# Scan convolutions on GpSimd and paired sampling weights in a four-stage vision kernel

## The chip, the cores and the metric

The kernel runs on one core of a Trainium2 chip. A core has TensorE (PE in the profile; PEld is its weight load), VectorE (DVE), ScalarE (ACT), GpSimd (POOL) and SyncE (SP), each with a queue of its own that it works through in order. They meet at semaphores only. Matrix products go to PSUM, eight banks of 512 float32 columns on 128 partitions; everything else lies in SBUF. GpSimd cannot read PSUM. The metric is device time in microseconds.

## The reference

Sixteen images of 64 channels and 16x16 pixels pass four layers, one after the other:

- L0: attention over channels. With q, k, v as 1x1 convolutions, `attn = softmax(scale * q @ k.T)` is 64x64 per image.
- L1: a modulated deformable 3x3 convolution. A 3x3 convolution gives two offsets and a mask for each of nine taps and each pixel; the image is sampled bilinearly at the shifted places, weighted with the mask and the convolution's weights, then batch norm and ReLU.
- L2: attention over the 256 pixels with a residual: `softmax(q.T @ k / 8)`, 256x256 per image.
- L3: a norm over the image, a 3x3 depthwise convolution giving `y`, then four scans added up, each `conv5(y) * sigmoid(g @ y)`: a depthwise convolution of five taps along rows (left to right, right to left) or along columns (both ways); a 1x1 convolution `fuse` with a residual; a second norm and a gated feed-forward layer with a residual.

## The kernel before

Images are worked in eight pairs n = 1 to 8, image 0 of a pair on partitions 0 to 63 and image 1 on 64 to 127, 256 pixels along the columns. All five engines' orders are written out by hand in `PLAN` (L53): a list of tokens `step.pair` for each of TensorE, ScalarE, VectorE and GpSimd, which `walk` (L147) plays in that order. Steps of up to four or five pairs are interleaved: while pair 4 is sampled, pair 1 is in its scans. A step waits for semaphores and issues its instructions. `turn` (L152) makes the users of a shared PSUM bank wait for the one before in the order of TensorE's list; bank `pair` (two banks) is used by wx, logit, gate, scan and ff, bank `mb` by the other small products.

The steps that the text names, by line:

- Front: qk, attn, at, mix and x1 are layer 0; x1 ends on VectorE in `x1_pad` (L863) and GpSimd copies it (L1033). off and off_t give the offsets, dist (L872), abs, hat (L877) and hat_y (L885) make triangular weights from them on VectorE and ScalarE; `high` (ScalarE) and `low` (GpSimd, L1039, five instructions) split them into two float16 parts, which tr0 to tr2 turn over on TensorE. wx0 to wx2 multiply the image with the convolution's weights.
- Sampling, nine taps per pair, 72 in all. `sp{k}` (L494, L489) spreads the row weights of a tap to PSUM bank yb0 (upper half of the image) and, for the tap before it, to yb1 (lower half), and the column weights to xb. ScalarE copies xb to SBUF (`xe`, L740). VectorE multiplies: `w{k}a` and `w{k}b` (L901), one instruction of 512 columns for each half of each tap, into a ring of six tiles. `s{k}a`, `s{k}b` (L534) multiply that with w_x into bank cv. After the last tap ScalarE's relu (L747) gives x2.
- Layer 2: qk2 (L547), v2, logit, max (L907), exp, nrm (L920), et, av, x3.
- Layer 3: st1 on VectorE and ln1 on GpSimd (five instructions on one column each, L1046 to L1055) make the norm, ScalarE writes `z_pad` (L785) and the first two depthwise taps, VectorE the other seven (dw2 to dw8, L942), and y (L951) adds the two sums into `y_pad`. gate (L602) and scan (L615) are TensorE's: the scan multiplies shifted views of `y_pad` with diagonal matrices, 2 axes x 5 taps x 2 images = 20 products, each two records in the trace. ScalarE adds the bias to `conv` (L808), prod (L957) multiplies with the gates, fuse, x4, st2, ln2, ff, u (L976), ff2 and out end the pair.
- `warm` and `hot` (L374, L380) are products of zeros, two per count, that keep TensorE at work at the start and after the last sampling.

Of the kernel before, what the change touches and what calls it, by code (L numbers as in the profile page):

```python
# [44 lines left out]
for _name, _n in PARTS:  # L45
# [29 lines left out]
        scan.5 sp3.8 tr2.8 s1a.8 qk2.7 s1b.8 sp4.8 s2a.8 fuse.5 sp5.8 logit.7 s2b.8 sp6.8 s3a.8 s3b.8 s4a.8 v2.7 s4b.8
        s5a.8 s5b.8 s6a.8 sp7.8 ff.5 et1.7 sp8.8 s6b.8 gate.6 et0.7 sp_last.8 s7a.8 av.7 s7b.8 s8a.8 s8b.8 ff2.5 scan.6
        qk2.8 hot.1 logit.8 fuse.6 hot.2 hot.3 v2.8 hot.4 et0.8 gate.7 et1.8 av.8 scan.7 hot.5 ff.6 fuse.7 gate.8 hot.6
        scan.8 ff2.6 hot.7 fuse.8 ff.7 hot.8 ff.8 ff2.7 hot.9 ff2.8
    """,
    "act": """  # L80
        attn.1 at.1 mix.1 off.1 prep.1 tanh.1 abs.1 attn.2 wx0.1 high.1 wx2.1 at.2 wx1.1 mix.2 tr0.1 xe0.1 tr1.1 xe1.1
        tr2.1 wx2.2 xe2.1 attn.3 halve.1 off.2 at.3 xe3.1 xe4.1 abs.2 mix.3 tanh.2 wx0.2 xe5.1 high.2 xe6.1 xe7.1 xe8.1
        tr0.2 attn.4 tr1.2 xe0.2 tr2.2 at.4 wx1.2 xe1.2 off.3 mix.4 relu.1 wx2.3 abs.3 wx0.3 tanh.3 xe2.2 xe3.2 high.3
        wx1.3 xe4.2 q2.1 k2.1 xe5.2 tr0.3 xe6.2 tr1.3 xe7.2 attn.5 xe8.2 tr2.3 xe0.3 v2.1 exp0.1 off.4 at.5 exp1.1 abs.4
        tanh.4 xe1.3 mix.5 xe2.3 et0.1 relu.2 wx0.4 et1.1 xe3.3 xe4.3 high.4 wx1.4 q2.2 k2.2 wx2.4 ln1.1 xe5.3 xe6.3
        dw.1 tr0.4 exp0.2 exp1.2 xe7.3 et0.2 xe8.3 v2.2 et1.2 tr1.4 xe0.4 xe1.4 tr2.4 gate.1 xe2.4 ln1.2 off.5 dw.2
        xe3.4 relu.3 scan.1 xe4.4 q2.3 k2.3 tanh.5 wx1.5 wx2.5 abs.5 wx0.5 xe5.4 ln2.1 high.5 v2.3 xe6.4 exp0.3 exp1.3
        xe7.4 tr0.5 ff.1 xe8.4 et1.3 gate.2 xe0.5 et0.3 xe1.5 tr1.5 ln1.3 relu.4 dw.3 attn.6 scan.2 q2.4 k2.4 xe2.5
        xe3.5 at.6 mix.6 tr2.5 exp0.4 exp1.4 xe4.5 wx2.6 off.6 xe5.5 ln2.2 wx1.6 v2.4 xe6.5 ff.2 abs.6 xe7.5 et0.4
        tanh.6 wx0.6 high.6 et1.4 xe8.5 tr0.6 gate.3 ln1.4 xe0.6 dw.4 scan.3 attn.7 tr1.6 xe1.6 relu.5 at.7 xe2.6 gate.4  # L90
        ln2.3 q2.5 k2.5 xe3.6 xe4.6 mix.7 scan.4 tr2.6 ff.3 xe5.6 off.7 abs.7 v2.5 xe6.6 tanh.7 wx0.7 high.7 xe7.6 wx1.7
        attn.8 wx2.7 xe8.6 tr0.7 at.8 mix.8 tr1.7 exp0.5 tr2.7 exp1.5 xe0.7 off.8 et0.5 xe1.7 relu.6 et1.5 xe2.7 wx0.8
        xe3.7 tanh.8 abs.8 wx2.8 ln1.5 q2.6 k2.6 xe4.7 wx1.8 dw.5 xe5.7 high.8 xe6.7 exp0.6 exp1.6 tr0.8 xe7.7 v2.6
        ln2.4 xe8.7 et1.6 xe0.8 et0.6 ff.4 xe1.8 relu.7 xe2.8 gate.5 ln1.6 dw.6 xe3.8 tr1.8 scan.5 xe4.8 q2.7 k2.7 tr2.8
        xe5.8 xe6.8 xe7.8 exp0.7 exp1.7 ln2.5 v2.7 ff.5 et1.7 xe8.8 et0.7 gate.6 ln1.7 relu.8 dw.7 scan.6 q2.8 k2.8
        exp0.8 v2.8 exp1.8 et0.8 et1.8 gate.7 ln2.6 ln1.8 dw.8 scan.7 ff.6 gate.8 ln2.7 scan.8 ff.7 ln2.8 ff.8
    """,
    "dve": """
        qk.1 a_max.1 a_norm.1 x1.1 dist.1 qk.2 a_max.2 hat.1 hat_y.1 a_norm.2 qk.3 low.1 x1.2 w0a.1 w0b.1 a_max.3 w1a.1
        a_norm.3 w1b.1 w2a.1 dist.2 w2b.1 w3a.1 hat.2 w3b.1 w4a.1 hat_y.2 x1.3 w4b.1 w5a.1 qk.4 w5b.1 w6a.1 w6b.1 w7a.1  # L100
        a_max.4 w7b.1 a_norm.4 w8a.1 w8b.1 w0a.2 dist.3 x1.4 w0b.2 w1a.2 hat.3 qk.5 hat_y.3 w1b.2 w2a.2 w2b.2 w3a.2
        w3b.2 w4a.2 w4b.2 w5a.2 a_max.5 w5b.2 w6a.2 w6b.2 w7a.2 max.1 a_norm.5 w7b.2 w8a.2 nrm0.1 dist.4 w8b.2 w0a.3
        nrm1.1 hat.4 w0b.3 w1a.3 hat_y.4 w1b.3 w2a.3 w2b.3 x3.1 st1.1 w3a.3 w3b.3 w4a.3 x1.5 w4b.3 w5a.3 max.2 dw3.1
        dw5.1 w5b.3 nrm0.2 w6a.3 nrm1.2 w6b.3 dw7.1 w7a.3 dw2.1 dw4.1 dw6.1 w7b.3 w8a.3 dw8.1 y.1 w8b.3 w0a.4 x3.2 st1.2
        w0b.4 w1a.4 w1b.4 w2a.4 dw2.2 dw4.2 dw6.2 dw8.2 dw3.2 dw5.2 dw7.2 dist.5 prod.1 w2b.4 y.2 x4.1 st2.1 w3a.4 hat.5
        hat_y.5 w3b.4 w4a.4 max.3 w4b.4 w5a.4 w5b.4 w6a.4 nrm1.3 nrm0.3 w6b.4 u.1 w7a.4 out.1 w7b.4 w8a.4 w8b.4 w0a.5
        x3.3 st1.3 qk.6 dw3.3 dw2.3 a_max.6 dw5.3 dw4.3 dw6.3 a_norm.6 dw7.3 w0b.5 w1a.5 prod.2 w1b.5 w2a.5 max.4 x1.6
        dw8.3 x4.2 st2.2 w2b.5 w3a.5 y.3 nrm0.4 w3b.5 w4a.5 dist.6 w4b.5 w5a.5 nrm1.4 u.2 w5b.5 hat.6 hat_y.6 out.2
        w6a.5 w6b.5 x3.4 st1.4 w7a.5 w7b.5 w8a.5 dw2.4 dw3.4 dw5.4 dw4.4 dw7.4 dw6.4 qk.7 dw8.4 y.4 a_max.7 prod.3 w8b.5
        w0a.6 a_norm.7 x4.3 st2.3 w0b.6 w1a.6 w1b.6 w2a.6 w2b.6 x1.7 w3a.6 w3b.6 u.3 w4a.6 out.3 dist.7 w4b.6 w5a.6  # L110
        hat.7 hat_y.7 qk.8 w5b.6 w6a.6 a_max.8 a_norm.8 max.5 w6b.6 w7a.6 w7b.6 x1.8 w8a.6 nrm0.5 prod.4 nrm1.5 w8b.6
        w0a.7 w0b.7 w1a.7 x3.5 dist.8 st1.5 x4.4 w1b.7 w2a.7 hat.8 w2b.7 w3a.7 hat_y.8 st2.4 w3b.7 w4a.7 max.6 w4b.7
# [1046 lines left out]
```

## Time and profile before

| | us |
|---|---|
| median of 3 runs (303.65, 303.65, 304.49) | 303.65 |
| span of the profiled execution, first to last instruction (the profile has no other time of it) | 301.8 |
| TensorE busy | 287.8 (95%) |
| VectorE busy | 213.0 (71%) |
| ScalarE busy | 190.4 (63%) |
| GpSimd busy | 53.0 (18%) |

Busy time is the union of an engine's instructions; TensorE's matmuls overlap and their ends are modelled, so the mean duration of one times the count is more than the busy time. An arrow in brackets behind an instruction names what ended the idle time before it. The share of the whole span hides that the first 28 and the last 46 us differ from the middle.

### The profile page before, as it was taken

What the parts mean: (1) busy time and instruction counts of PE and PEld (TensorE: products, weight loads), DVE (VectorE), ACT (ScalarE), POOL (GpSimd) and SP (SyncE); (2) the same over time, 40 slices, a digit from 0 to 9 for tenths busy, and PEclk for the clock granted to TensorE, in tenths of its full rate; (3) what the DMA queues carried; (4) which work ended last, traced back from release to release, by engine and by line L of the source; (5) the groups of instructions that cost most, each with busy time, mean ns of one, the idle gap of its engine ahead of it and who ended that gap; (6) DMA issues with size and microseconds to landing.
All of it is one profiled execution on the core that took longest, in us unless ns stands there. A gap on an engine that the chain in (4) does not pass through costs nothing.

```text
span 301.8 us, 7399 instructions
## 1 busy us (share of the span) xinstructions
PE 287.8 (95%) x2870; PEld 183.7 (61%) x2870; DVE 213.0 (71%) x424; ACT 190.4 (63%) x399; POOL 53.0 (18%) x139
## 2 busy tenths in 40 slices
...
DMA packets 3057, 4.98 MB, mean 16 GB/s; under 512 B 336, under 2 KB 2768, under 8 KB 2896
## 3 DMA queue, kind: packets, MB, share of 16 engines
...
HBM read 3.47 MB, written 1.05 MB: 15 GB/s over the span
## 4 chain that ended last, share of the span: by engine, by line
PE 85%; DVE 5%; ACT 5%; issue 3%; POOL 1%; ACTq 0%; POOLq 0%; DVEq 0%
PE ps_cv L534 22%; PE ps_pair L615 11%; PE ps_yb L494 8%; PE ps_pair L480 7%; PE ps_ma L437 6%; PE ps_ma L464 4%; PE ps_mb L580 3%; PE ps_pair L602 3%; PE ps_pair L570 3%; PE ps_mb L591 3%; PE ps_mb L547 3%; PE ps_mb L388 2%; PE ps_pair L635 2%; PE ps_mb L624 2%; PE ps_yb L374 1%
## 5 line engine op out<-in xcount | busy, mean ns | idle before, releaser
L901 DVE TENSOR_TENSOR sb_wt<-ps_yb,sb_xe 128x512 f32<-128x512 f32 x144 | 94.0, 684 | 26.4 <-PE ps_xb L489 24.9
L534 PE MATMUL ps_cv<-sb_wt,sb_w_x 128*64 128x256 f32 x576 | 77.3, 385 | 0.0
L740 ACT ACTIVATE sb_xe<-ps_xb 128x512 f32<-128x512 f32 x72 | 43.0, 597 | 19.3 <-PE ps_xb L489 19.2
L534 PEld LDWEIGHTS ps_cv<-sb_wt,sb_w_x 128*64 128x64 f32 x576 | 38.2, 136 | 20.2 <-issue 7.5
L615 PE MATMUL ps_pair<-sb_y_pad,sb_par 64*128 64x256 f32 x320 | 37.4, 383 | 0.3 <-ACT sb_gates L799 0.3
L615 PEld LDWEIGHTS ps_pair<-sb_y_pad,sb_par 64*128 64x128 f32 x320 | 30.9, 184 | 5.8 <-issue 2.5
L942 DVE SCALAR_TENSOR_TENSOR sb_dw_acc<-sb_z_pad,sb_par,sb_dw_acc 128x256 f32<-128x256 f32 x56 | 25.2, 480 | 9.4 <-ACT sb_dw_acc L792 5.3
L494 PE MATMUL ps_yb<-sb_hats,sb_sel 32*128 32x512 f16 x144 | 29.8, 383 | 0.7
L1039 POOL TENSOR_TENSOR sb_parts<-sb_hat,sb_parts 128x256 f16<-128x256 f32 (+2 forms) x40 | 23.3, 615 | 38.7 <-ACT sb_parts L710 38.6
L1046 POOL TENSOR_SCALAR sb_sc<-sb_mv 128x1 f32<-128x1 f32 x16 | 3.0, 190 | 142.1 <-DVE sb_mv L936 74.7
L489 PE MATMUL ps_xb<-sb_hats,sb_sel 32*128 32x512 f16 x72 | 27.7, 385 | 0.2 <-ACT sb_hats L719 0.2
L730 ACT ACTIVATE sb_w_x<-ps_pair 128x1024 f32<-128x1024 f32 (+1 forms) x24 | 19.4, 810 | 7.7 <-PE ps_pair L480 7.5
L480 PE MATMUL ps_pair<-sb_par,sb_x 64*128 64x256 f32 (+1 forms) x192 | 23.4, 361 | 0.6 <-ACT sb_w_x L730 0.3
L719 ACT ACTIVATE sb_hats<-ps_ma 128x1024 f16<-128x1024 f16 (+1 forms) x24 | 21.1, 880 | 1.7 <-PE ps_ma L464 1.5
L494 PEld LDWEIGHTS ps_yb<-sb_hats,sb_sel 32*128 32x128 f16 x144 | 7.3, 91 | 21.2 <-issue 17.0
L480 PEld LDWEIGHTS ps_pair<-sb_par,sb_x 64*128 64x128 f32 x192 | 15.5, 185 | 7.3 <-issue 6.7
L808 ACT ACTIVATE sb_conv<-ps_pair,sb_par 128x512 f32<-128x512 f32 x16 | 10.1, 683 | 13.1 <-PE ps_pair L615 13.0
L437 PE MATMUL ps_ma<-sb_x_pad,sb_par 128*64 128x128 f32 x288 | 17.4, 274 | 0.3 <-ACT sb_hats L719 0.3
L437 PEld LDWEIGHTS ps_ma<-sb_x_pad,sb_par 128*64 128x64 f32 x288 | 15.8, 136 | 2.3 <-issue 1.6
L769 ACT ACTIVATE sb_b_exp<-ps_pair,sb_b_neg 128x256 f32<-128x256 f32 x32 | 14.8, 473 | 3.0 <-DVE sb_b_neg L910 2.7
L872 DVE TENSOR_TENSOR sb_dist<-ps_ma,sb_grid 128x1152 f32<-128x1152 f32 x8 | 10.8, 1354 | 6.2 <-PE ps_ma L446 6.2
L464 PE MATMUL ps_ma<-sb_sel,sb_parts 128*64 128x128 f16 x320 | 13.8, 222 | 0.0
...
## 6 DMA issues: line engine op xcount, KB each, us to landing
...
sb_x_in<-in_x SPq DMA_DIRECT2D x8, 128.0 KB, 2.1
out_y<-sb_y_out SPq DMA_DIRECT2D x8, 128.0 KB, 1.7
...
sb_par<-in_par SPq DMA_DIRECT2D x1, 128.0 KB, 2.2
sb_sel<-in_sel SPq DMA_DIRECT2D x1, 128.0 KB, 3.9
```

The costliest lines, as they stand in the source:

```text
L437: mm = nc.tensor.matmul(ma[C * h:C * (h + 1), 0:P], par_sb[:, a + 2 * OM * t:a + 2 * OM * (t + 1)], x1_pad[:, r:r + HALF_ROWS, t % 3:t % 3 ...
L464: mm = nc.tensor.transpose(bk[columns_of(t), at:at + P], parts[:, 2 * h + b, 4 * g + 2 * t:4 * g + 2 * (t + 1), :, :], ident16)
L480: mm = nc.tensor.matmul(pair[:, 512 * b + PIX * h:512 * b + PIX * h + k], x1[r, P * h:P * (h + 1)], par_sb[r, a:a + k], start=True, stop=True)
L489: return nc.tensor.matmul(xb[:, :], sel_sb[rows, P:2 * P], hats[n % 2][rows, g, :], start=True, stop=True)
L494: return nc.tensor.matmul(yb[h][:, :], sel_sb[rows, P * (2 + h):P * (3 + h)], hats[n % 2][rows, g, :], start=True, stop=True)
L534: mm = nc.tensor.matmul(cv[C * b:C * (b + 1), 0:PIX], w_x[n % 2][:, b, h, k, :], wt_of(n, k, h)[:, PIX * b:PIX * (b + 1)], start=(k == 0 a ...
L615: mm = nc.tensor.matmul(pair[:, 512 * b + PIX * d:512 * b + PIX * (d + 1)], par_sb[r, a:a + P], rows, start=(j == 0), stop=(j == KS - 1))
L719: nc.scalar.activation(hats[n % 2][:, g0:g1, :].rearrange("p g q -> p (g q)"), ma[:, :].bitcast(F16)[:, 0:k], ACT.Copy).then_inc(ev(f"hats ...
L740: nc.scalar.activation(xe[t % XE][:, :], xb[:, :], ACT.Copy).then_inc(ev("xe_ok"), 1)
L901: nc.vector.tensor_tensor(wt_of(n, k, h)[:, :], yb[h][:, :], xe[t % XE][:, :], ALU.mult)\
L942: nc.vector.scalar_tensor_tensor(out=sum_of, in0=dw_source(t), scalar=col("dw_w", t), in1=sum_of, op0=ALU.mult, op1=ALU.add).then_inc(ev(f ...
L1039: nc.gpsimd.tensor_tensor(parts[:, 0:g, a:b, 1, :], hat[:, 0:g, a:b, :], parts[:, 0:g, a:b, 0, :], ALU.subtract).then_inc(ev("low_ok"), 1)
```

## The change

- The scans of pairs 1 to 6 move from TensorE to GpSimd; pairs 7 and 8 keep theirs. For a pair in `BY_POOL`, y goes to a plain tile, SP's queue copies it with four DMAs to `y_dup` (each direction of a scan needs both images, and its two ways lie on the two halves of the partitions), and GpSimd works per axis d: a multiply-add with the middle tap and the bias, then four multiplies into a temporary, each followed by an addition. gate reads the plain tile.
- The two halves of a tap no longer have a bank each. Tap t has bank t % 2, and `w{k}` multiplies in one instruction the lower half of the tap before and the upper half of this one: 128 x 1024 from two banks. The ring has four tiles of twice the size, xe four parts instead of three.
- Many tiles get a second or third buffer, with explicit waits where the order alone held before.
- All orders are written anew, SP's too (it was a loop of stores and loads). In TensorE's list scan.1 to scan.6 are gone and the counts of `hot` are 26 instead of 46.

```diff
-RING = 6
-HOT = {1: 4, 2: 2, 3: 3, 4: 2, 5: 5, 6: 5, 7: 8, 8: 13, 9: 4}
+RING = 4
+BY_POOL = (1, 2, 3, 4, 5, 6)
+ORDER = (2, 1, 3, 0, 4)
+SUMS = 2 * KS - 1
+HOT = {1: 1, 2: 2, 3: 1, 4: 3, 5: 1, 6: 3, 7: 3, 8: 1, 9: 4, 10: 4, 11: 3}
-XE = 3
+XE = 4
...
     "pool": """
+        grid.1 x1.1 low.1 x1.2 low.2 x1.3 bn.1 low.3 x1.4 ln1.1 low.4 mul00.1 mul01.1 sum01.1 mul10.1 mul02.1 mul11.1
...
+        ln2.1 mul00.2 mul10.2 mul11.2 mul01.2 sum11.2 sum01.2 mul12.2 mul02.2 ln1.3 sum02.2 mul03.2 sum03.2 mul04.2
+        sum12.2 mul13.2 sum13.2 mul14.2 sum04.2 sum14.2 x1.6 mul00.3 mul10.3 mul01.3 mul11.3 sum11.3 sum01.3 mul02.3
+        ln2.2 mul12.3 sum02.3 sum12.3 mul03.3 mul13.3 sum03.3 low.6 ln1.4 sum13.3 mul04.3 mul14.3 sum04.3 sum14.3 ln2.3
...
+    "sp": """
+        load.3 load.4 load.5 dup.1 load.6 load.7 dup.2 dup.3 load.8 store.1 dup.4 store.2 dup.5 dup.6 store.3 store.4
+        store.5 store.6 store.7 store.8
...
+            def dup(n):
+                sp.wait_ge(ev("y_ok"), n)
+                for d in range(2):
+                    wait_past(sp, ev(f"scan_step{d}"), SUMS * made_by(BY_POOL, n - 2))
+                for b in range(2):
+                    for i in range(2):
+                        sp.dma_start(y_dup[n % 2][C * i:C * (i + 1), b, :, :].rearrange("p h w -> p (h w)"),
+                                     y[n % 2][C * b:C * (b + 1), :])\
+                            .then_inc(dup_ok[n % 2], 16)
...
-                nc.vector.tensor_tensor(wt_of(n, k, h)[:, :], yb[h][:, :], xe[t % XE][:, :], ALU.mult)\
-                        .then_inc(ev("wt_ok"), 1)
+                    dve.wait_ge(ev("sp_mm"), spread_of(n, k))
+                    dve.wait_ge(ev("xe_ok"), t)
+                    wait_past(dve, ev("smp_mm"), 2 * (t - RING) - 1)
...
+                    nc.vector.tensor_tensor(wt[:, join_of(n, k, 0) % RING, :, :], yb[:, :].rearrange("p (s q) -> p s q", s=2),
+                                            xe[:, even:odd + 1:odd - even, :], ALU.mult).then_inc(ev("wt_ok"), 1)
...
             def prod_step(n):
+                wait_past(dve, ev("fuse_mm"), n - 2)
                 dve.wait_ge(ev("gate_ok"), n)
-                dve.wait_ge(ev("scan_ok"), n)
+                if n in BY_POOL:
+                    for d in range(2):
+                        dve.wait_ge(ev(f"scan_step{d}"), scan_step(n, d, SUMS - 1))
...
+            def scan_rows(n, d, j):
+                at, to = max(0, j - KS // 2), max(0, KS // 2 - j)
+                m = H - at - to
...
+            def scan_times(d, i):
+                def step(n):
+                    rows, sum_of, tap_to = scan_rows(n, d, ORDER[i])
+                    weight = col("scan_c", KS * d + ORDER[i])
+                    if i == 0:
+                        pool.wait_ge(dup_ok[n % 2], 64 * len([k for k in BY_POOL if k <= n and (n - k) % 2 == 0]))
+                        wait_past(pool, ev("prod_ok"), n - 2)
+                        nc.gpsimd.tensor_scalar(sum_of, rows, weight, col("scan_b", d), ALU.mult, ALU.add)\
+                            .then_inc(ev(f"scan_step{d}"), 1)
+                    else:
+                        pool.wait_ge(ev(f"scan_step{d}"), scan_step(n, d, 2 * i - 2))
+                        nc.gpsimd.tensor_scalar(tap_to, rows, weight, None, ALU.mult).then_inc(ev(f"scan_step{d}"), 1)
+                return step
+
+            def scan_plus(d, i):
+                def step(n):
+                    rows, sum_of, tap_to = scan_rows(n, d, ORDER[i])
+                    pool.wait_ge(ev(f"scan_step{d}"), scan_step(n, d, 2 * i - 1))
+                    nc.gpsimd.tensor_tensor(sum_of, sum_of, tap_to, ALU.add).then_inc(ev(f"scan_step{d}"), 1)
+                return step
```

In VectorE's new order y.1 stands between w4.3 and w5.3 (before, between w8a.3 and w8b.3), prod.6 amid the dw steps of pair 7 and ahead of max.8, and prod.7 behind y.8 (before, amid the dw steps of pair 8).

## Rows read from the trace of the kernel before

**Rows 1.** The page: its head, and the chain that ended last by engine and line

```profile
span 301.8 us, 7399 instructions
PE 85%; DVE 5%; ACT 5%; issue 3%; POOL 1%; ACTq 0%; POOLq 0%; DVEq 0%
PE ps_cv L534 22%; PE ps_pair L615 11%; PE ps_yb L494 8%; PE ps_pair L480 7%; PE ps_ma L437 6%; PE ps_ma L464 4%; PE ps_mb L580 3%; PE ps_pair L602 3%; PE ps_pair L570 3%; PE ps_mb L591 3%; PE ps_mb L547 3%; PE ps_mb L388 2%; PE ps_pair L635 2%; PE ps_mb L624 2%; PE ps_yb L374 1%
```

**Rows 2.** Busy time by stretch: stretch, length, engines in the order PE, PEld, DVE, ACT, POOL

```profile
28.00:97.00 69.00, 67.82 (x749) 42.53 (x747) 55.40 (x106) 50.90 (x111) 10.85 (x22) 1.00 0.01 4
97.00:255.50 158.50, 157.46 (x1562) 101.26 (x1556) 125.95 (x248) 108.01 (x225) 28.30 (x76) 1.00 0.03 7
255.50:302.00 46.50, 40.02 (x330) 26.08 (x328) 21.31 (x46) 19.48 (x39) 6.73 (x24) 1.00 0.04 13
...
210.00:240.00 30.00, 29.97 (x285) 17.72 (x283) 27.96 (x58) 23.60 (x48) 7.14 (x20) 1.00 0.02 6
```

**Rows 3.** The chain in order of time, pair 6's scan: start, length

```profile
255.56 4.61 PE ps_pair L615 x40
```

**Rows 4.** Groups by line, TensorE: count, busy us, mean ns, idle before

```profile
L615 PE MATMUL ps_pair<-sb_y_pad,sb_par 64*128 64x256 f32 x320 | 37.4, 383 | 0.3 <-ACT sb_gates L799 0.3
...
L380 PE MATMUL ps_xb<-sb_idle 128*64 128x512 f16 x92 | 11.4, 381 | 0.0
```

**Rows 5.** Groups by line, VectorE

```profile
L901 DVE TENSOR_TENSOR sb_wt<-ps_yb,sb_xe 128x512 f32<-128x512 f32 x144 | 94.0, 684 | 26.4 <-PE ps_xb L489 24.9
L942 DVE SCALAR_TENSOR_TENSOR sb_dw_acc<-sb_z_pad,sb_par,sb_dw_acc 128x256 f32<-128x256 f32 x56 | 25.2, 480 | 9.4 <-ACT sb_dw_acc L792 5.3
...
L907 DVE TENSOR_REDUCE sb_b_max<-ps_pair 128x4 f32<-128x1024 f32 x8 | 9.7, 1217 | 1.9 <-PE ps_pair L570 1.9
```

**Rows 6.** Groups by line and shape, GpSimd

```profile
L1039 POOL TENSOR_TENSOR sb_parts<-sb_hat,sb_parts 128x256 f16<-128x256 f32 x28 | 18.2, 680 | 34.1 <-ACT sb_parts L710 34.0
...
L1033 POOL COPY sb_x<-sb_x_pad 128x256 f32<-128x256 f32 x8 | 3.4, 421 | 54.8 <-DVE sb_x_pad L863 40.1 <-PE ps_pair L480 14.7
...
L1055 POOL TENSOR_TENSOR sb_sc<-sb_par,sb_sc 128x1 f32<-128x1 f32 x16 | 3.0, 190 | 1.3
L1024 POOL TENSOR_TENSOR sb_grid<-sb_par 128x1152 f32<-128x1152 f32 x1 | 2.1, 2150 | 0.0
...
L1019 POOL TENSOR_SCALAR sb_bn_s<-sb_bn_s,sb_par 128x1 f32<-128x1 f32 x1 | 0.3, 340 | 0.1
```

**Rows 7.** Instructions in order of time, VectorE and GpSimd side by side: start, length

```profile
30.69 0.25 DVE L856 TENSOR_SCALAR sb_a_nrm<-sb_a_exp,sb_a_rec 128x64 f32<-128x64 f32 x1
...
112.84 0.76 DVE L877 TENSOR_SCALAR sb_hat<-sb_hat 128x1152 f32<-128x1152 f32 x1 [0.29 <-ACT sb_hat L704]
112.93 0.72 POOL L1051 TENSOR_TENSOR sb_sc<-sb_sc,sb_par 128x1 f32<-128x1 f32 x1
...
142.91 0.47 DVE L942 SCALAR_TENSOR_TENSOR sb_dw_acc<-sb_z_pad,sb_par,sb_dw_acc 128x256 f32<-128x256 f32 x1
143.05 0.58 POOL L1033 COPY sb_x<-sb_x_pad 128x256 f32<-128x256 f32 x1 [12.08 <-DVE sb_x_pad L863]
...
192.74 2.31 POOL L1039 TENSOR_TENSOR sb_parts<-sb_hat,sb_parts 128x256 f16<-128x256 f32 x4
...
193.94 0.76 DVE L856 TENSOR_SCALAR sb_a_nrm<-sb_a_exp,sb_a_rec 128x64 f32<-128x64 f32 x1
```

**Rows 8.** Instructions in order of time, after the last sampling matmul

```profile
256.85 0.60 ACT L785 ACTIVATE sb_z_pad<-sb_x,sb_sc 128x256 f32<-128x256 f32 x1 [3.09 <-POOL sb_sc L1055]
257.36 0.55 ACT L747 ACTIVATE sb_x<-ps_cv,sb_bn_s 128x256 f32<-128x256 f32 x1
...
260.11 1.08 PE L547 MATMUL ps_mb<-sb_x,sb_par 128*64 128x256 f32 x8
```

**Rows 9.** DMA issues: size, median us from issue to landing

```profile
sb_x_in<-in_x SPq DMA_DIRECT2D x8, 128.0 KB, 2.1
```

**Rows 10.** VectorE's first work behind the memsets

```profile
6.19 0.69 DVE L840 TENSOR_TENSOR sb_qk<-ps_mb,sb_par 128x512 f32<-128x512 f32 x1 [3.43 <-PE ps_mb L388]
```

More of the change, by code:

```diff
@@ L75 @@
[L75 to L78, printed above, removed]
+        warm.1 warm.2 warm.3 warm.4 qk.1 attn.1 warm.5 at.1 mix.1 x1.1 off.1 prep.1 off_t.1 qk.2 warm.6 attn.2 qk.3
@@ L83 @@
[L83 to L96, printed above, removed]
+        attn.1 at.1 mix.1 off.1 prep.1 tanh.1 abs.1 attn.2 high.1 wx0.1 at.2 tr0.1 mix.2 xe0.1 wx2.1 xe1.1 tr1.1 xe2.1
@@ new lines @@
+        tr1.7 mix.8 xe0.7 tr2.7 exp0.5 exp1.5 off.8 et0.5 xe1.7 et1.5 tanh.8 xe2.7 abs.8 xe3.7 relu.6 ln1.5 dw.5 wx0.8
+        high.8 wx2.8 q2.6 xe4.7 k2.6 wx1.8 xe5.7 v2.6 tr0.8 xe6.7 exp0.6 exp1.6 xe7.7 tr1.8 et1.6 xe8.7 et0.6 xe0.8
+        xe1.8 ln1.6 dw.6 ln2.4 relu.7 xe2.8 ff.4 xe3.8 q2.7 k2.7 gate.5 xe4.8 xe5.8 tr2.8 exp0.7 exp1.7 xe6.8 v2.7 ln2.5
+        xe7.8 et1.7 et0.7 xe8.8 ff.5 gate.6 ln1.7 dw.7 relu.8 q2.8 k2.8 v2.8 exp0.8 exp1.8 et0.8 et1.8 gate.7 ln2.6
+        ln1.8 dw.8 scan.7 ff.6 gate.8 scan.8 ln2.7 ff.7 ln2.8 ff.8
@@ L97 @@
     """,
     "dve": """
[L99 to L112, printed above, removed]
```

309 lines of the change are left out of this document (193 added, 116 removed).

## The prediction

> **What bounds the kernel now.** I read the chain of waits first, then the stretches, then the costliest groups. The chain [rows 1] is to be read by engine: 85% of a span of 301.8 us is TensorE, and L615, the scan convolution, alone is 11%. The stretches [rows 2] say where: from 28 us (first sampling matmul) to 255.5 us (after the last one) TensorE is busy 67.8 of 69 and 157.5 of 158.5 us. So there the time is the sum of what is in TensorE's queue; nothing else ends last. Before 28 us and after 255.5 us the engines wait for one another. VectorE is second: 55.4 + 126.0 = 181.4 of those 227.5 us, and 27.96 of 30 (93%) at 210 to 240 us, the fullest that it gets. GpSimd has 28.3 of 158.5 us. The granted clock is 1.00 throughout, the 2.4 GHz level.
>
> **Scans off TensorE.** A scan is 40 records of L615, 37.4 us for eight pairs [rows 4]; the one of pair 6 fills 4.61 us of the chain [rows 3]. Six go. Five stand between 28 and 255.5 us: 5 x 4.61 = 23.1 us off a full queue. Pair 6's stands behind the last sampling matmul, ahead of qk2.8, which could start once relu.8 is done. relu.8 ran at 257.36, behind ln1.7 at 256.85, and qk2.8 at 260.11 [rows 8]. Without the scan qk2.8 goes at some 258.1 (257.36 + 0.55 + 0.2), or 256.4 if relu.8 comes at once: 2.0 to 3.7 us. The twelve ScalarE copies that fed from it go too; ScalarE is not on the path, so I count nothing. prod.7 now stands behind y.8 instead of amid the dw steps of pair 8: 1.2 us off the last chain at most (a wide VectorE instruction takes that, rows 5). Tail together 2.0 to 4.9 us; I take 3.5.
>
> If all else kept up, that is a floor: 301.8 - 23.1 - 4.9 = 273.8 us of span. The three timed runs have a median of 303.65, 1.85 above the span; I add that to each result (the profiled execution has no time of its own beside its span): 275.7.
>
> **Weights in one instruction over two banks.** Before: 144 instructions, 94.0 us busy, 653 ns each [rows 5]. After: 71 of twice the width and two single ones. The nearest row of that width from PSUM is L907 with 1217 ns; with the overlap of ends that the 684 and 653 ns of L901 show, 1190. 71 x 1.19 + 2 x 0.68 = 85.9: VectorE saves 8.1 us. Bounds: 0 (1.3 us each) and 18 (only the columns paid, 1.05). As VectorE is second, this buys no time by itself; it pays for the next term. The wait for a weight pair is now one 1.2 us instruction that both the spread step and two sampling steps stand behind; TensorE has other work between them, so I cost it at nothing while VectorE is not late.
>
> **Scans on GpSimd.** Per pair and axis: one multiply-add and four multiplies on 512, 480, 480, 448, 448 columns and four sums on the last four. No row shows them. Sums: two inputs, 680 ns at 256 columns and 2150 at 1152 [rows 6], so 1.64 ns a column, 1.10, 1.05 and 1.00 us: 8 per pair make 8.2 us. Multiplies: the copy of 256 columns takes 421 ns and an instruction on one column 190 [rows 6], so 0.91 ns a column; two operands read per partition made 340 of 190, so 75 ns each: 0.80, 0.70, 0.67 us, 7.1 us per pair. Upper end: the price of a two-input instruction, 10.4 us; lower, the copy alone, 6.4. A scan is 15.3 us (14.6 to 18.6), six are 92 us (88 to 112).
>
> The copies that feed it (four DMAs per pair in SP's queue, behind y) land like an input load, 2.1 us [rows 9]; a pair waits one such latency, covered by the other pairs' work (uncovered, 6 x 2.1 = 12.6 us). They are queued ahead of load.6, load.8 and the stores: load.6 stood behind store.1 before, later than dup.1 now, and nobody waits for the stores of pairs 1 to 4 until two pairs later. Nothing.
>
> **What the two engines do to each other.** This decides. GpSimd's instruction on one column, 0.19 us [rows 6], took 0.72 us where it met VectorE's hat step of 0.76 us [rows 7]; its copy of 0.42 took 0.58 us behind a dw step. And VectorE's a_nrm, 0.25 us alone, took 0.76 us in the middle of GpSimd's row of low steps, of 0.58 us each [rows 7]. So each waits for the other with such instructions. L901, which reads PSUM and one tile, is never lengthened: it stays at 684 in the mean [rows 5]. VectorE instructions of the kind that meet (two inputs in SBUF, or one and none in PSUM) are, per pair, seven dw steps, y, prod, u, hat, hat_y, a_nrm and four of nrm. Today they rarely meet GpSimd; after, GpSimd is busy 92 + 28 of some 150 us (from y.1, where the second stretch of rows 2 begins and three taps earlier in the new order, to prod.6).
>
> VectorE's price: a_nrm lost 0.51 us to a step of 0.58. A scan step is 0.85 us (15.3/18), so a dw step behind one waits up to 0.65, say 0.6 in a row of dw steps, and others half of that. By the new orders on the two engines the dw steps of pairs 3 and 6 lie wholly beside a scan, those of 2, 4, 5, 7 partly: some 25 of 42, 15 us; of the 60 others half, 0.3 each: 9. So 24 us. Ends: 0 (GpSimd always at a wait when they come) and 42 x 0.65 + 60 x 0.33 = 47. I take 24, the middle, as a_nrm was one row of its kind.
>
> VectorE then has 181.4 - 8.1 + 24 = 197.3 us of work between first and last sampling; at the 93.2% of its fullest stretch that takes 211.7 us, against 227.5 before and 204.4 by TensorE's queue. So VectorE becomes the bound there: -15.8 us instead of -23.1. Span 301.8 - 15.8 - 3.5 = 282.5, time 284.3: I predict **284**.
>
> GpSimd's price: 0.18 to 0.5 us per meeting, some 55 meetings, 18 us: 92 + 28 + 18 = 138 of 150 us. Near its end too, but not yet the bound.
>
> The Trainium skill, SBUF - State Buffer, Who interferes with whom, says that a VectorE instruction with two SBUF inputs, or in a two-port mode, and a GpSimd instruction that reads SBUF exclude each other for the whole instruction. The trace agrees in kind (0.19 to 0.72 us), but shows 0.18 us lost behind a 0.47 us dw step, as the copy had begun 0.14 us after it and has a start-up of its own; taken whole it would be 0.33 us, GpSimd's price an estimated 26 us instead of 18 and its load 146 of 150 us, so by that rule rival 3 below is nearer than I have it.
>
> **The rest.** Deeper buffers: the added waits on earlier pairs (n-1, n-2, n-3) are for steps that ended long before in their queues; nothing, and where a wait of n-1 became n-2 nothing either, as TensorE's queue was full. Two more memsets go ahead of VectorE's first work, which waits 3.43 us for TensorE [rows 10]: nothing, and 0.7 us if it did not. Filler matmuls after the last sampling fall from 46 to 26 pairs of 92 records, 11.4 us busy [rows 4]; they fill waits. If the clock fell for lack of them, TensorE's part of the tail (40.0 busy less 11.4 of filler) would double at 1.2 GHz, at most 28 us; all rows show 1.00, so I take 0.
>
> **Rivals.**
> 1. VectorE and GpSimd seldom meet (the new orders place dw steps where GpSimd waits), TensorE stays the bound: 275.7. For it: TensorE is full now, and GpSimd itself has waits ahead of ln1, low and x1. Against: dw.3 and dw.6 lie amid scans.
> 2. They meet more: 35 us on VectorE: 208.3/0.932 = 223.5, so -4.0 - 3.5, span 294.3, time 296. For it: a row of dw steps makes GpSimd's next step go first each time.
> 3. GpSimd becomes the bound, the slower side. Its scan stands ahead of x1, low, ln1 and ln2 of other pairs, and prod.n stands in VectorE's queue ahead of later weights, max and nrm. At 18.6 us a scan and 27 us of meetings it has 112 + 28 + 27 = 167 us, at 93% 180 us, where the floor leaves 143: 273.8 + 37 = 311, time 312. It decides from a demand of some 160 us on: a scan of 17.5 us with those meetings. Against: a multiply reads one tile, so it should be nearer to the copy than to the two-input row.
> 4. No change: the losses happen to equal the gain, 303.
>
> **How the numbers follow.** Forecast 45%, rival 1 25%, rival 2 15%, rival 3 10%, rival 4 5%. Faster by over 0.3% (what a measurement of this kernel can tell; its three runs lie 0.84 us apart, with two equal) are the first three: 85%; of rival 4 most lies within 0.3%: 4%; slower 11%. The range goes from just below rival 1, 274, to above rival 2, 299; the forecast's own is 279 to 290.
>
> **What would show it.** Right: L615 with 80 records; GpSimd's busy time at some 150 us or more; L901 near 1.2 us; dw steps well over their 480 ns [rows 5]; VectorE over 90% full between first and last sampling, and TensorE idle behind weights there. Wrong: dw still at 480 ns and TensorE at 99% (rival 1); prod waiting for GpSimd for microseconds and x1, low or ln1 late (rival 3); scan steps far from 0.7 and 1.05 us; a granted clock under 1.00 in the tail.

## The result, and the profile after

The changed kernel takes 345.52 us (median of four runs, 344.44 to 346.71) against 304.07 (303.65 to 304.51) for the kernel before beside it: a ratio of 1.137, 95% interval 1.1335 to 1.140. It is 41 us slower, where 284 us was forecast.

The page after: span, busy time by engine, and the granted clock in 40 slices.

```profile
span 342.7 us, 6942 instructions
...
PE 277.1 (81%) x2590; PEld 163.7 (48%) x2590; DVE 222.4 (65%) x355; ACT 184.9 (54%) x387; POOL 193.5 (56%) x247
...
PEclk9699999999999859969679998999999899789998
```

TensorE issues fewer matmuls, but it is no longer full, and its granted clock (PEclk, in tenths of full speed) has holes. The chain that ended last, by engine and by line, answers to [rows 1]:

```profile
POOL 39%; PE 33%; DVE 10%; issue 10%; ACT 3%; DMA 3%; SPq 2%; DVEq 0%; POOLq 0%; ACTq 0%
POOL sb_tap_of L1157 18%; POOL sb_conv L1164 11%; PE ps_cv L574 7%; PE ps_pair L520 3%; POOL sb_conv L1153 3%; PE ps_ma L477 3%; PE ps_pair L656 3%; PE ps_yb L534 3%; DMA sb_y_dup<-sb_y 3%; DVE sb_dw_acc L1007 2%; POOL sb_sc L1125 2%; DVE sb_wt L956 2%; PE ps_ma L504 2%; SPq L382 2%; PE ps_yb L414 1%
```

TensorE fell from 85% of the chain to 33%; GpSimd rose from 1% to 39%, and L1157, the scan's multiplies, is the largest line. Three stretches (before the first sampling matmul, up to the last, after it; columns as in [rows 2], then the granted clock, the DMA share and GB/s) tell where:

```profile
0.00:32.00 32.00, 24.23 (x236) 15.28 (x238) 11.71 (x28) 11.71 (x27) 5.64 (x13) 0.89 0.29 93
32.00:292.60 260.60, 217.26 (x2114) 126.84 (x2110) 189.84 (x283) 154.90 (x324) 173.38 (x204) 0.93 0.05 11
292.60:342.70 50.10, 35.60 (x252) 21.59 (x248) 20.84 (x46) 18.32 (x37) 14.49 (x31) 0.90 0.03 11
```

Before, these stretches were 27.9, 226.9 and 47.0 us long. Of the 41 us, 4 lie ahead of sampling, 34 in it, 3 behind it. In the middle TensorE is busy 217 of 261 us (225 of 227 before), VectorE 190, GpSimd 173. The groups of GpSimd by line and shape, and of the two lines of VectorE that answer to [rows 5]:

```profile
L1157 POOL TENSOR_SCALAR sb_tap_of<-sb_y_dup,sb_par 128x480 f32<-128x480 f32 x24 | 38.0, 1586 | 0.8
L1157 POOL TENSOR_SCALAR sb_tap_of<-sb_y_dup,sb_par 128x448 f32<-128x448 f32 x24 | 35.1, 1466 | 0.8
L1164 POOL TENSOR_TENSOR sb_conv<-sb_conv,sb_tap_of 128x480 f32<-128x480 f32 x24 | 28.6, 1203 | 0.5
L1164 POOL TENSOR_TENSOR sb_conv<-sb_conv,sb_tap_of 128x448 f32<-128x448 f32 x24 | 27.2, 1144 | 0.6
...
L1153 POOL TENSOR_SCALAR sb_conv<-sb_y_dup,sb_par 128x512 f32<-128x512 f32 x12 | 10.2, 855 | 22.5 <-DMA sb_y_dup<-sb_y 22.5
...
L956 DVE TENSOR_TENSOR sb_wt<-ps_yb,sb_xe 128x1024 f32<-128x1024 f32 x71 | 86.6, 1220 | 17.1 <-PE ps_xb L529 17.0
...
L1007 DVE SCALAR_TENSOR_TENSOR sb_dw_acc<-sb_z_pad,sb_par,sb_dw_acc 128x256 f32<-128x256 f32 x56 | 30.3, 585 | 27.3 <-ACT sb_dw_acc L838 27.1
```

The odd one is L1157: a multiply of 480 columns takes 1586 ns, and the multiply-add of 512 columns, L1153, takes 855. The scan of a pair is 139 / 6 = 23.2 us where 15.3 was worked out. The middle stretch begins long before the first scan. From GpSimd's first scan step to its last, and in a piece of that:

```profile
97.00:302.00 205.00, 158.58 (x1392) 89.06 (x1390) 140.44 (x213) 108.22 (x224) 169.59 (x187) 0.90 0.04 11
138.10:193.70 55.60, 43.31 (x369) 24.09 (x365) 36.64 (x57) 26.70 (x57) 53.54 (x57) 0.85 0.04 10
```

GpSimd is busy 83% of the first and 96% of the second, where TensorE has 78%: there GpSimd's own work is the bound. Elsewhere the engines wait for one another. The waits (total, times, longest):

```profile
ACT sb_z_pad L833 <- POOL sb_sc L1131: 32.2, 8, 9.9
...
DVE sb_dw_acc L1007 <- ACT sb_dw_acc L838: 27.1, 7, 9.2
POOL sb_conv L1153 <- DMA sb_y_dup<-sb_y: 22.5, 4, 9.4
...
PE ps_mb L665 <- DVE sb_prod L1029: 19.9, 6, 11.1
...
DVE sb_prod L1029 <- POOL sb_conv L1164: 13.3, 5, 4.8
```

Read from the bottom: TensorE's fuse waits for VectorE's product, that for GpSimd's sums; GpSimd's next scan waits for copies of the next y; y waits for the depthwise taps; those for ScalarE's z, and z for the layer norm's statistics (L1131), which stand in GpSimd's queue amid the scan of the pair ahead. It is a ring through GpSimd, ScalarE, VectorE and SyncE's copies, on which TensorE's fuse hangs. The chain in order of time shows one turn (start, length). From fuse to y it goes through what stands next in the queues of TensorE and VectorE (logit, max, weights, taps):

```profile
119.72 0.19 POOL sb_sc L1131
119.91 1.39 POOL sb_tap_of L1157
...
122.83 1.24 DVE sb_prod L1029
...
124.11 1.97 PE ps_mb L665 x8
...
132.96 0.34 DVE sb_y L1019
...
134.47 0.60 SPq L382
...
135.11 2.89 DMA sb_y_dup<-sb_y
...
138.09 1.53 POOL sb_conv L1153 x2
...
139.71 2.96 POOL sb_tap_of L1157 x2
```

From the end of y (133.3) to the first scan step (138.1) 4.8 us pass, as SyncE issues the copies one after another (SPq).

### The profile page after: what moved, and what is told of

The parts are those of the page before. It is cut to its first block, busy times and chain, and to the rows that moved or that the text cites. A ratio compares the mean times of both kernels' runs of the same rounds, so it can differ in the third digit from the quotient of the medians.

```text
span 342.7 us, 6942 instructions
## 1 busy us (share of the span) xinstructions
PE 277.1 (81%) x2590; PEld 163.7 (48%) x2590; DVE 222.4 (65%) x355; ACT 184.9 (54%) x387; POOL 193.5 (56%) x247
## 3 DMA queue, kind: packets, MB, share of 16 engines
HBM read 3.47 MB, written 1.05 MB: 13 GB/s over the span
## 4 chain that ended last, share of the span: by engine, by line
POOL 39%; PE 33%; DVE 10%; issue 10%; ACT 3%; DMA 3%; SPq 2%; DVEq 0%; POOLq 0%; ACTq 0%
POOL sb_tap_of L1157 18%; POOL sb_conv L1164 11%; PE ps_cv L574 7%; PE ps_pair L520 3%; POOL sb_conv L1153 3%; PE ps_ma L477 3%; PE ps_pair L656 3%; PE ps_yb L534 3%; DMA sb_y_dup<-sb_y 3%; DVE sb_dw_acc L1007 2%; POOL sb_sc L1125 2%; DVE sb_wt L956 2%; PE ps_ma L504 2%; SPq L382 2%; PE ps_yb L414 1%
## 5 line engine op out<-in xcount | busy, mean ns | idle before, releaser
L956 DVE TENSOR_TENSOR sb_wt<-ps_yb,sb_xe 128x1024 f32<-128x1024 f32 x71 | 86.6, 1220 | 17.1 <-PE ps_xb L529 17.0
L574 PE MATMUL ps_cv<-sb_wt,sb_w_x 128*64 128x256 f32 x576 | 83.7, 398 | 6.0 <-issue 5.9
L1157 POOL TENSOR_SCALAR sb_tap_of<-sb_y_dup,sb_par 128x480 f32<-128x480 f32 (+1 forms) x48 | 73.0, 1526 | 1.6
L1164 POOL TENSOR_TENSOR sb_conv<-sb_conv,sb_tap_of 128x480 f32<-128x480 f32 (+1 forms) x48 | 55.7, 1173 | 1.1
L574 PEld LDWEIGHTS ps_cv<-sb_wt,sb_w_x 128*64 128x64 f32 x576 | 36.9, 140 | 29.1 <-issue 18.6
L1007 DVE SCALAR_TENSOR_TENSOR sb_dw_acc<-sb_z_pad,sb_par,sb_dw_acc 128x256 f32<-128x256 f32 x56 | 30.3, 585 | 27.3 <-ACT sb_dw_acc L838 27.1
L520 PE MATMUL ps_pair<-sb_par,sb_x 64*128 64x256 f32 (+1 forms) x192 | 24.7, 377 | 5.1 <-POOL sb_x L1109 2.7
L665 PE MATMUL ps_mb<-sb_prod,sb_fuse_h 128*64 128x256 f32 x64 | 9.5, 422 | 19.9 <-DVE sb_prod L1029 19.9
L1153 POOL TENSOR_SCALAR sb_conv<-sb_y_dup,sb_par 128x512 f32<-128x512 f32 x12 | 10.2, 855 | 22.5 <-DMA sb_y_dup<-sb_y 22.5
L833 ACT ACTIVATE sb_z_pad<-sb_x,sb_sc 128x256 f32<-128x256 f32 x8 | 4.8, 604 | 32.2 <-POOL sb_sc L1131 32.2
L477 PE MATMUL ps_ma<-sb_x_pad,sb_par 128*64 128x128 f32 x288 | 19.4, 292 | 0.8 <-DVE sb_x_pad L915 0.8
L1029 DVE SCALAR_TENSOR_TENSOR sb_prod<-sb_gates,sb_conv 128x1024 f32<-128x1024 f32 x8 | 10.3, 1287 | 13.7 <-POOL sb_conv L1164 13.3
```

The source lines that it names most:

```text
L477: mm = nc.tensor.matmul(ma[C * h:C * (h + 1), 0:P], par_sb[:, a + 2 * OM * t:a + 2 * OM * (t + 1)], x1_pad[:, r:r + HALF_ROWS, t % 3:t % 3 ...
L520: mm = nc.tensor.matmul(pair[:, 512 * b + PIX * h:512 * b + PIX * h + k], x1[r, P * h:P * (h + 1)], par_sb[r, a:a + k], start=True, stop=True)
L574: mm = nc.tensor.matmul(cv[C * b:C * (b + 1), 0:PIX], w_x[n % 2][:, b, h, k, :], wt_of(n, k, h)[:, PIX * b:PIX * (b + 1)], start=(k == 0 a ...
L956: nc.vector.tensor_tensor(wt[:, join_of(n, k, 0) % RING, :, :], yb[:, :].rearrange("p (s q) -> p s q", s=2), xe[:, even:odd + 1:odd - even ...
L1007: nc.vector.scalar_tensor_tensor(out=sum_of, in0=dw_source(n, t), scalar=col("dw_w", t), in1=sum_of, op0=ALU.mult, op1=ALU.add).then_inc(e ...
L1157: nc.gpsimd.tensor_scalar(tap_to, rows, weight, None, ALU.mult).then_inc(ev(f"scan_step{d}"), 1)
```

## The experiments

Medians; "before" was 303.4 to 303.6 us in each set.

**e1, the form or the shape of the multiply.**

```diff
-  tensor_scalar(tap_to, rows, weight, None, ALU.mult)
+  pairs 1, 5: as it was;  pairs 2, 6: (rows, weight, 0.0, mult, add);  pair 3: (rows, weight, 1.0, mult, mult)
+  pair 4: as it was, on all 512 columns in one run
```

> The changed kernel with the multiplies of the scans in other forms by pair: pairs 1 and 5 as they are (one operation, product with the weight), 2 and 6 with a second operation (+ 0.0), 3 with a second operation (x 1.0), 4 one operation but over all 512 columns in one run. Theory 'form': one operation alone is the slow form (1.40 to 1.48 us undisturbed); pairs 2, 3 and 6 take 0.70 to 0.76 us, pair 4 about 1.55 us; the time falls by some 30 us as half the scans shrink by 6 us each. Rival 'shape': what is slow are the 14 or 15 wide pieces and 2 x 240 rows instead of one run of 512; then pairs 2, 3 and 6 stay at 1.4 to 1.5 us and pair 4 takes 0.76 us.

One run, 334.27 us: 11 us less than the change, where some 30 was expected. The multiplies: 512 columns flat (L1164), one operation (L1158), two with "+ 0.0" (L1160):

```profile
L1164 POOL TENSOR_SCALAR sb_tap_of<-sb_y_dup,sb_par 128x512 f32<-128x512 f32 x8 | 13.0, 1626 | 0.4
L1158 POOL TENSOR_SCALAR sb_tap_of<-sb_y_dup,sb_par 128x480 f32<-128x480 f32 x8 | 12.6, 1580 | 0.3
L1158 POOL TENSOR_SCALAR sb_tap_of<-sb_y_dup,sb_par 128x448 f32<-128x448 f32 x8 | 11.8, 1475 | 0.1
...
L1160 POOL TENSOR_SCALAR sb_tap_of<-sb_y_dup,sb_par 128x480 f32<-128x480 f32 x8 | 6.1, 774 | 0.2
L1160 POOL TENSOR_SCALAR sb_tap_of<-sb_y_dup,sb_par 128x448 f32<-128x448 f32 x8 | 5.5, 689 | 0.5
```

The form decides: the same columns cost half with a second operation (pair 3, with "x 1.0", has 0.76 us on 480 and 0.93 on 448 columns in the mean, and a median of 0.66 over both). That the rows are cut into short runs does not: flat, it is as dear.

**e2, GpSimd nearly free.** The four outer taps of pairs 1 to 6 are left out.

```diff
-  mul00.1 mul01.1 sum01.1 mul10.1 ... sum14.1   (18 steps a pair)
+  mul00.1 mul10.1                               (2 steps a pair)
```

> The changed kernel with GpSimd doing the middle tap and the bias alone, so the other four taps of the scans of pairs 1 to 6 are left out (2 of 18 instructions per pair stay). Theory 'GpSimd is the bound': without its 128 us the rest runs as I forecast for the floor, 275 to 282 us, TensorE full again from 28 us on and the granted clock 1.00. Rival 'order': if the new order, the buffers or the paired weights cost time by themselves, it stays above 300 us.

291.87 us (ratio 0.959, 0.9555 to 0.963). The sampling stretch:

```profile
32.00:246.80 214.80, 206.54 (x2112) 123.84 (x2109) 178.11 (x284) 156.41 (x327) 55.92 (x118) 0.99 0.05 14
```

So the outer taps cost 53.7 us; but with GpSimd at 56 of 215 us there it is still 16 above the floor of 275.7, between the theory and its rival. Of the 16, 4 lie ahead of sampling (it begins at 32.0 and not at 27.9 us), 11 in it (214.8 for 226.9 - 23.1) and 1 behind it.

**e3, all scans back on TensorE, in the new order.**

```diff
-  "pe": ... gate.1 ... fuse.1        BY_POOL = (1, 2, 3, 4, 5, 6)
+  "pe": ... gate.1 ... scan.1 ...    BY_POOL = ()
```

> The changed kernel with all scans back on TensorE and nothing of them on GpSimd or SP: new order, deeper buffers and paired weights alone (the six scan steps are put behind gate in TensorE's and ScalarE's lists). Theory 'GpSimd is the bound': 298 to 306 us, about the kernel before, as TensorE's work is the same. Rival 'order': over 310 us.

326.52 us (1.073, 1.066 to 1.080), as the rival said. Part of it is my placing: a scan right behind its gate waits for ScalarE's gates, which before cost 0.3 us [rows 4]:

```profile
PE ps_pair L608 <- ACT sb_gates L799: 6.3, 7, 1.6
```

**e4, e6, e9: the order before, scans on TensorE, deeper buffers.** e4 has the wide weights; e6 two narrow ones side by side, each with its own signal; e9 each narrow one at its own place in VectorE's order, as before.

```diff
e4  w5b.3 nrm0.2 w6a.3  ->  nrm0.2 w6.3          (one instruction over two banks)
e6  w6.3 = for u in (t - 1, t): tensor_tensor(...).then_inc(wt_ok, 1)
e9  w5b.3 nrm0.2 w6a.3                           (as before)
```

> The kernel before with the paired weights and the deeper buffers, its own order and filler, all scans on TensorE. Paired weights save VectorE some 8 us; TensorE is the bound, so 302 to 305 us. If the wait for both halves at once hurts the sampling loop: 306 to 312 us, with TensorE idle behind weights.

> The kernel before's order and its scans on TensorE, with the deeper buffers, but the sampling weights made by two narrow instructions per pair of taps, each giving its own signal (310.9 us with one wide instruction, 303.6 before). Theory 'the wide instruction makes TensorE wait': the first half of a pair of taps comes a narrow instruction's time later, so that TensorE's gaps go from 1 to 6 us and the rest is the clock; with two narrow ones the time is back at 302 to 305 us. Rival 'deeper buffers': the weights' form costs nothing and the buffers, which change what is due when, cost the 7 us; the time stays at 309 to 312 us.

> The kernel before's order with the deeper buffers and all scans on TensorE, and the narrow weights each at its own place in VectorE's order, as before (308.6 us with the two of a join side by side, 303.6 before). Theory 'the join': what costs TensorE time is that the older half waits for its partner's place in VectorE's order, so that in its own place the time is back at 302.5 to 304.5 us and TensorE waits under 1 us for weights. Rival 'deeper buffers': their bank and their counts cost the 5 us; the time stays at 307 to 310 us.

310.89 (1.023, 1.021 to 1.026), 308.64 (1.0165, 1.014 to 1.019) and 304.54 us (1.004, 1.002 to 1.006). e4 is in its second range, e6 between its two, e9 at the upper end of its theory. TensorE's waits for weights in e4:

```profile
PE ps_cv L512 <- DVE sb_wt L894: 3.6, 6, 1.3
...
PE ps_yb L472 <- DVE sb_wt L894: 1.2, 4, 0.5
```

and in e6:

```profile
PE ps_yb L472 <- DVE sb_wt L895: 1.8, 6, 0.5
PE ps_cv L512 <- DVE sb_wt L895: 1.2, 2, 0.8
```

e9 has none of 0.4 us or more. The deeper buffers cost 1 us; that the older half waits for its partner's place 4.1; that both come in one instruction 2.3 more. The rival "deeper buffers" of e6 falls.

**e5, the cheap multiply in the changed kernel.**

```diff
-  tensor_scalar(tap_to, rows, weight, None, ALU.mult)
+  tensor_scalar(tap_to, rows, weight, 0.0, ALU.mult, ALU.add)
```

> The changed kernel, with each of GpSimd's 48 multiplies given a second operation that changes nothing (times the tap, plus 0.0). Theory 'price of the form': the one-operation multiply measured 1.40 to 1.48 us undisturbed and the two-operation one 0.64 to 0.66 in the probe, so 48 of them at about 0.70 in place of 1.53 take 40 us off GpSimd (193.5 to about 154, some 16.4 us of scan per pair in place of 23.2). GpSimd then has room in a pair's 30 us, the stretches behind it go, and the time falls to 296 to 308 us (the floor here is 291.9, what the kernel took with the middle tap alone on GpSimd). Rival 'the order': pairs come in an order that stalls whatever GpSimd costs; the time stays at 320 us or above, with GpSimd's busy time down. Rival 'GpSimd still the bound': with 154 us of work in windows where it waits for VectorE's weights and for its own copies, the chain still shows GpSimd at 25% or more, time 312 to 325 us.

322.52 us (1.062, 1.060 to 1.065): 23 us less than the change, so the price of the form is real, but above the theory's 296 to 308 and in the ranges of both rivals. GpSimd's busy time is 155.8 us, as worked out; the chain still has it at 24%, just under the sign of the second rival. The sampling stretch, VectorE's depthwise taps and ScalarE's wait for statistics:

```profile
32.30:274.50 242.20, 217.49 (x2110) 128.08 (x2108) 192.64 (x283) 155.34 (x326) 139.73 (x210) 0.94 0.05 12
...
L1007 DVE SCALAR_TENSOR_TENSOR sb_dw_acc<-sb_z_pad,sb_par,sb_dw_acc 128x256 f32<-128x256 f32 x56 | 38.4, 729 | 14.8 <-ACT sb_dw_acc L838 14.6
...
ACT sb_z_pad L833 <- POOL sb_sc L1131: 19.2, 8, 4.7
```

Against e2, with the same TensorE work (2110 and 2112 matmuls), TensorE idles 24.7 in place of 8.3 us, and is busy 217.5 in place of 206.5 us at a granted clock of 0.94 in place of 0.99: 16.4 + 11.0 = 27.4, the whole difference of the two stretches.

**e7, e8: e5 with two narrow weights; then also TensorE's start as before.**

```diff
e7  w4.1 = for u in (t - 1, t): tensor_tensor(...).then_inc(wt_ok, 1)
e8  also  warm.1 warm.2 warm.3 warm.4 qk.1 attn.1  ->  warm.1 warm.2 qk.1 attn.1 warm.3 at.1 warm.4
```

> The changed kernel with two-operation multiplies on GpSimd and with the weights as two narrow instructions per pair of taps. Theory 'both count, and VectorE has room': the weights' early half gives TensorE 4 to 7 us, so 4 to 7 us below the kernel with two-operation multiplies alone. Rival 'VectorE is the bound': 71 wide instructions become 142 narrow ones at about 0.68 us, 10 us more of VectorE work (210 to 220 us in 240), which stalls its later work; the time is the same as with the wide ones or up to 8 us above it.

> As the kernel with two-operation multiplies and narrow weights, with TensorE's first stage in the order of before (two fillers ahead of the first product of queries and keys in place of four). Theory 'the start is late by 4 us': the first sampling began at 27.9 us before and at 32.0 after, so the time falls by 3 to 4 us. Rival 'the start is hidden': VectorE or GpSimd has the last word later on, and the time moves by under 1 us.

320.83 and 318.19 us (1.055 and 1.048): 1.7 and 2.6 us won, each less than its theory. With GpSimd in the chain the early half of the weights is worth less than in the order before. The late start is not hidden, but e8 brings back only part of it: its first sampling matmul is at 30.6 us, 32.4 in e7 and 27.9 before.

**e10 to e14: a few scans on GpSimd in the order before** (e9 as the base, cheap multiplies): pairs 2 and 4; 2, 3 and 4, with fuse.3 and what follows it later; 4 alone; and the first two with GpSimd's order mended (e14 has e13's change too).

```diff
e10  low.5 [scan.2, 8 steps] ln1.3 [scan.2, 7 steps] x1.6      e13  low.5 [scan.2, 15 steps] ln1.3 x1.6
e11  [scan.3] ln2.3 [scan.4] x1.7 ... low.7 x1.8               e14  [scan.3] x1.7 ... low.7 ln2.3 ... x1.8
e12  ln2.3 [scan.4, 10 steps] x1.7 [scan.4, 8 steps] low.7
```

> The same, with the scans of pairs 2 and 4 alone on GpSimd, with two-operation multiplies. In the kernel before these two pairs have 33 and 42 us between their y and their fuse on TensorE, so that a scan of 16 us and its copies of 3 us fit in with nothing moved. Theory 'a scan pays where the order gives it the time': TensorE loses 2 x 3.9 us of scan and nothing waits for GpSimd, so 6 to 8 us below the same order without them (296 to 298 us if that is at 303.6). Rival 'GpSimd's work costs what it saves': VectorE's meetings with it (17 us over six scans) and the late copies hold TensorE, and the time is within 2 us of the same order without them.

> As the kernel with pairs 2 and 4, with pair 3 too, whose fuse and what follows it are moved some 13 us later (behind the next pair's offsets) to give its scan time. Theory: another 3 to 4 us off TensorE, so 9 to 12 us below the same order without scans on GpSimd (292 to 295 us). Rival 'VectorE's queue': GpSimd runs three scans on end from 115 to 190 us, beside the sampling weights, and pair 3's product, placed by hand, stalls VectorE; the time is at or above that of pairs 2 and 4 alone.

> The order of before with narrow weights in place (304.5 us), with the scan of pair 4 alone on GpSimd, two-operation multiplies. Pair 4 has 42 us between y and fuse. Theory 'the place decides': in the run with pairs 2 and 4 the stretch of pair 4 ran 2 to 3 us shorter than before, so one scan there gives 2 to 4 us: 300.5 to 302.5 us. Rival 'meetings': each scan costs VectorE about 3 us of meetings and these hold TensorE; the time is 304 us or more.

> Pairs 2 and 4 on GpSimd, with pair 2's scan run to its end before GpSimd turns to pair 3's statistics (before, it waited 7 us for them in the middle of the scan, and the whole came to 308.5 us). Theory 'the place decides': the 7 us wait and the stall of TensorE behind it go, 297 to 301 us. Rival 'meetings': in pair 2's stretch GpSimd's sums meet VectorE's normalisation (one of 2.14 us in place of 0.35) and its depthwise taps (up to 1.28 in place of 0.48), with TensorE waiting for both; the wait in the middle was only a consequence, and the time stays at 305 to 310 us.

> Pairs 2, 3 and 4 on GpSimd, with no statistics that come late placed ahead of GpSimd's copies for the next pairs (339 us with them there, with TensorE waiting up to 13 us for such a copy). Theory 'the place decides': that wait goes, and the time is at most that of pairs 2 and 4 mended, 294 to 300 us. Rival 'meetings': 50 us of scans on end beside VectorE's work; 305 us or more.

308.51, 339.05, 303.43, 307.75 and 334.09 us (ratios 1.016, 1.117, 0.999, 1.015, 1.102). Only pair 4 alone does no harm: its median is 1.1 us below its base, with runs from 301.57 to 305.32, and against the kernel before its interval is 0.9963 to 1.002, no change that can be told and less than its theory. None of the five beats the kernel before; the theories of e10, e11, e13 and e14 failed.

The mending of e13 gave 0.8 us: its rival was right. VectorE's normalisation of pair 3 (four instructions, 1.2 us together in the kernel before), from 119 to 128 us of e13:

```profile
L914 DVE TENSOR_SCALAR sb_b_nrm<-sb_b_exp,sb_b_rec 128x256 f32<-128x256 f32 x4 | 4.5, 1166 | 0.1
```

and what TensorE waited for from 100 to 150 us:

```profile
PE ps_mb L528 <- ACT sb_a_exp L659: 4.2, 1, 4.2
PE ps_mb L561 <- DVE sb_b_nrm L914: 1.8, 1, 1.8
PE ps_mb L625 <- DVE sb_ff_u L980: 1.7, 1, 1.7
```

In e9 these waits are below 0.4 us. So three microseconds of meetings become 7.7 us of TensorE's idle time, because the normalisation feeds everything up to pair 3's y, and a_neg, on which a_exp waits, stands behind the depthwise taps in VectorE's queue. The scan that was taken off was worth 4.7 (37.4 / 8, [rows 4]). In e11 one copy behind late statistics in GpSimd's queue held TensorE:

```profile
PE ps_pair L461 <- POOL sb_x L1038: 13.3, 1, 13.3
```

e14 moved it: a gap of 6.6 us that e11 has too stayed, and one of 6.7 us came in its place.

## Why the prediction was wrong, point by point

The sum of the steps from before to after, each from one run to the next: deeper buffers 303.6 to 304.5 (+0.9, e9), joined weights to 310.9 (+6.4, e4), the new order to 326.5 (+15.6, e3), scans on GpSimd at the forecast price to 322.5 (-4.0, e5), the multiply's real price to 345.5 (+23.0). In e3 I put the scans back right behind their gates, and the 6.3 us of waits there are that placing; so the 15.6 is a bound on the order, not its price. Another way goes round e3: from the floor of 275.7 to e2 +16.2 (order, joined weights, start), to e5 +30.6 (the outer taps on GpSimd at the forecast price), to the change +23.0. The forecast had 8.6 for the first two together.

**Step "Scans on GpSimd", the multiplies: failed.** I took 0.70 and 0.67 us from a copy plus 75 ns an operand, with 1.05 and 1.00 as the upper end; it is 1.59 and 1.47. The nearest row was the wrong kind: nothing before shows a one-operation TENSOR_SCALAR with a per-partition scalar on GpSimd, and I took a two-input row as the ceiling though nothing says that it is one. With two operations the price is 0.69 and 0.74 us (e5), as worked out. The sums were 15% dearer (1.20 and 1.14 us for 1.05 and 1.00), so that a scan in e5 is (34.1 + 55.4 + 9.4) / 6 = 16.5 us, inside the 14.6 to 18.6 forecast. This term is 23 of the 61 us between forecast and result. (The lower end of the multiplies adds up to 6.2 us a pair, not 6.4, which changes nothing.)

**Step "What the two engines do to each other", the bound: failed.** I made VectorE's sum, at a fullness of 93%, the bound. VectorE is 73% full in the sampling stretch (189.8 of 260.6 us), TensorE 83%. In the change GpSimd is the bound where scans stand back to back (96% from 138.1 to 193.7 us). With the price as forecast (e5) no engine's sum is the time: from the first scan step to the last GpSimd is busy 72%:

```profile
96.60:279.40 182.80, 156.85 (x1394) 89.50 (x1396) 146.30 (x213) 108.73 (x228) 131.85 (x187) 0.93 0.05 13
```

The sampling stretch of e5 is 242.2 us where I had 211.7. What I called covered "by the other pairs' work", the latency of a pair, is by the chain what is left as the bound: y, copies (4.8 us in the turn shown, where I had 2.1), scan, with the next pair's statistics in GpSimd's queue amid the scan, then its taps and its y. How much of that ring is queueing and how much the meetings that lengthen its links, no run here separates.

**Meetings: right in kind, smaller in size, but on the path.** VectorE's busy time rose by 222.4 - 210.1 (e4) = 12 us, and 18 with cheap multiplies; I had 24 of 0 to 47. VectorE was not over 90% full, and TensorE's idle time stood behind prod, not behind weights, against both of my signs. I priced them by VectorE's sum, and e13 shows the price in TensorE's idle time, twice and more.

**Weights: right for the instruction, wrong in price.** 86.6 us and 1220 ns for 85.9 and 1190; but VectorE as a whole wins 3.9 us (214.0 busy in e9, 210.1 in e4) where I had 8.1. The wait for a pair of weights, which I cost at nothing, is 6.4 us with TensorE full (e9 to e4). "TensorE has other work between them" was wrong there: it had none ready by order.

**Scans off TensorE: nearly right.** L656 has 80 records; with GpSimd nearly free (e2) TensorE is busy 19 us less in the sampling stretch, at a clock of 0.99 (23 forecast), and the tail is 43.2 us, 3.8 shorter (3.5 forecast).

**"The rest": wrong where I counted nothing.** The start is 4.1 us later; bringing back 1.8 of it gave 2.6 at the end (e8). The clock, which I took as 1.00, fell in all three stretches: 0.89, 0.93 and 0.90. In the tail the fewer fillers are not enough to explain it, as e2 with the same ones has 0.98 there. It fell where TensorE idled: without a matmul for 11 us while it waits for prod.1, then at half speed (1.2 GHz), then back:

```profile
113.10:124.10 11.00, 0.00 (x0) 0.00 (x0) 1.76 (x3) 4.12 (x8) 9.10 (x12) 0.71 0.00 0
124.10:127.90 3.80, 3.79 (x16) 1.95 (x16) 2.32 (x5) 0.65 (x1) 3.07 (x5) 0.50 0.00 0
127.90:148.40 20.50, 17.39 (x175) 9.72 (x173) 15.89 (x28) 11.38 (x24) 12.21 (x16) 1.00 0.06 14
```

Over the sampling stretch that is 10.7 us of longer matmuls for the same work (217.3 against 206.5 in e2).

**Rivals.** Rival 3 named the place (scan ahead of x1, low, ln1 and ln2, prod ahead of later weights) and its point of decision, a scan of 17.5 us; it is 23.2. In the change it holds where GpSimd is full. I gave it 10% and 312 us; it came to 345. Its "against" leaned on the very row that failed. With 16.5 us, below that point, the outer taps still cost 30.6 us (e2 to e5), so the point was wrong too.
